# A graph layer on one Trainium2 core: the products of A2 behind the next unit's z, and the second score unit of a group between its third and fourth pair of row products

## The reference, cut to what matters

```python
h = relu(layernorm(x))
q, k, v = h @ Wq + bq, h @ Wk + bk, h @ Wv + bv
eh = edge_attr_64 @ We + be
attn_in = concatenate([q[src], k[dst], eh], axis=-1)
hmid = leaky_relu(attn_in @ A1 + b1, 0.2)
scores = leaky_relu(hmid @ A2 + b2, 0.2)        # 8 heads
w = softmax(scores.mean(axis=-1), axis=0)       # over all edges
out = segment_sum(w[:, None] * v[dst], src, num_segments=12500)
x + layernorm(h @ Wn + bn + out) * gamma + beta
```

## Time and profile before

| | |
|---|---|
| median of 3 runs | 6567.2 us (6549.49 to 6578.67) |
| the profiled execution | 6557.52 us, span 6555.7 us |
| PE, DVE, POOL, ACT busy | 76%, 63%, 49%, 46% of the span |
| mean granted clock of PE | 0.862 of full |

### The profile page before, as it was taken

How to read it: one execution, slowest core, us unless ns; L and a number is a source line. 1 busy time by engine, 2 the same in 40 slices (tenths; PEclk the granted TensorE clock), 3 DMA queues, 4 the chain that set the end, 5 groups by cost and what they waited for, 6 DMA issues and landing times. The chain is left out here.

```text
span 6555.7 us, 137361 instructions
## 1 busy us (share of the span) xinstructions
PE 4960.7 (76%) x35449; PEld 3918.0 (60%) x35449; DVE 4109.7 (63%) x9779; ACT 3008.6 (46%) x7687; POOL 3185.0 (49%) x3381
## 2 busy tenths in 40 slices
PE   7545456777878788788888887888878878879955
PEld 4433345656666666666666666666666666666754
DVE  7444444556656666566666665666666666656689
ACT  4223233444544445454445554555444445553455
POOL 3665565545555555555555555555555555520011
PEclk9777777888888888888898888888888888889999
DMA  8566666777777776666666766666666666647877
GB/s 234 151 194 201 194 190 202 210 206 212 220 218 213 224 218 187 176 194 193 188 189 193 197 192 180 190 195 195 181 182 181 190 183 192 198 134 204 229 175 184
DMA packets 1938653, 1276.41 MB, mean 195 GB/s; under 512 B 637802, under 2 KB 1830929, under 8 KB 1938444
## 3 DMA queue, kind: packets, MB, share of 16 engines
q1 hardware_dynamic: 1768101, 831.59, 50.3%
q0 software_dynamic: 154752, 435.99, 18.3%
q10 hardware_dynamic: 15592, 6.41, 0.4%
HBM read 703.28 MB, written 570.23 MB: 194 GB/s over the span
## 5 line engine op out<-in xcount | busy, mean ns | idle before, releaser
L1284 POOL DMA_INDIRECT slots<-rows,slot_i x3224 | 3098.9, 961 | 2566.4 <-ACT rows L1442 1169.9
L1339 PE MATMUL ps_row<-win,mixed 128*128 128x256 f32 x5904 | 1543.2, 406 | 150.0 <-ACT rows L1442 63.6
L1442 ACT ACTIVATE rows<-ps_row 128x512 f32<-128x512 f32 x1476 | 886.3, 600 | 1008.2 <-remote 668.6
L857 ACT ACTIVATE low<-ps_z 128x512 f32<-128x512 f32 (+1 forms) x882 | 517.9, 587 | 1801.9 <-remote 1065.7
L1339 PEld LDWEIGHTS ps_row<-win,mixed 128*128 128x128 f32 x5904 | 1127.8, 202 | 333.3 <-issue 133.7
L869 DVE TENSOR_SCALAR onehot<-ps_ls,part 128x512 bf16<-128x512 bf16 x686 | 330.3, 482 | 1429.2 <-remote 583.1
L789 PE MATMUL ps_ls<-mid,a_at 128*32 128x128 f32 x5488 | 365.3, 361 | 650.1 <-issue 524.4
L1498 ACT ACTIVATE early_v<-early_v,early_weight 128x128 f32<-128x128 f32 x2744 | 835.7, 393 | 6.1 <-DMA early_v<-slots 6.0
L1310 PE MATMUL ps_e<-ident,edges 128*128 128x128 f32 x3224 | 559.1, 298 | 361.5 <-DMA edges<-edge_attr_dram 139.6
L776 PE MATMUL ps_z<-onehot,q_bits 128*128 128x512 bf16 (+1 forms) x2646 | 795.3, 410 | 41.8 <-issue 40.2
L1310 PEld LDWEIGHTS ps_e<-ident,edges 128*128 128x128 f32 x3224 | 449.8, 157 | 587.9 <-issue 306.1
(11 more groups left out here) (220 smaller groups left out, 5177.0 us busy)
## 6 DMA issues: line engine op xcount, KB each, us to landing
u_rows<-slots SPq DMA_DIRECT2D x820, 258.0 KB, 3.2
early_v<-slots SPq DMA_DIRECT2D x686, 258.0 KB
edges<-edge_attr_dram SPq DMA_DIRECT2D x403, 256.0 KB
q_bits<-qb_tab SPq DMA_DIRECT2D x882, 96.0 KB, 3.0
slots<-no_row SPq DMA_DIRECT2D x98, 528.0 KB
slots<-rows,slot_i POOLq DMA_INDIRECT x3224
slots<-no_row SPq DMA_DIRECT2D x98, 396.0 KB
u_rows<-slots SPq DMA_DIRECT2D x134, 193.5 KB, 2.8
```

The source lines that it names most:

```text
L857: nc.scalar.activation(o.low[:, k % n, 0:w, :], o.ps_z[:, k % o.ps_z.shape[1], 0:w, :], ACT.Copy, scale=SLOPE).then_inc(o.low_ready, 1)
L1284: pool.indirect_dma_start(slots_tab[h], bass.IndirectOffsetOnAxis(slot_i[:, u, j:j + 1], 0), rows[:, u, j, :], None).then_inc(scattered[u] ...
L1339: last = pe.matmul(bank[:, j % 2, :], mixed[:, u % 2, j, :], win[:, u, :], start=True, stop=True)
L1442: nc.scalar.activation(rows[:, u, 2 * k:2 * k + 2, 0:2 * U0].rearrange("p j (a c) -> p j a c", a=2)[:, :, :, 0:D], row_bank(s, k).rearrang ...
```

## The change

In the loop over groups the batch's A2 products move from ahead of spread_lo to behind make_z of the same unit, and count on a semaphore of their own (`heads_made0`), for which raise_heads and leaky_z wait. DVE takes leaky_z ahead of one_of in the unit after a batch. On PE and on ACT the late unit moves between pair 2 and pair 3. The last batch's counts follow.

```diff
         def heads_count(o, i, k):
             if o.inside:
-                i, k = unit_of(o, i, k)
-                return i * o.units + k // BATCH * BATCH + (batch_size(o, i, k) + 2)
+                return batch_at(o, i, k) + 1
...
-                       low_ready=sem("low_ready0"), mid_ready=sem("mid_ready0"), s_ready=unit_made,
+                       low_ready=sem("low_ready0"), mid_ready=sem("mid_ready0"), s_ready=sem("heads_made0"),
...
                     def unit(i, k):                                  # PE
-                        if ended(o, i, k - 1):
-                            batch_heads(pe, o, *ended(o, i, k - 1))
                         if has_unit(o, i, k + 1):
                             spread_lo(pe, o, *unit_of(o, i, k + 1))
                         if ended(o, i, k - 2):
                             sum_heads(pe, o, *ended(o, i, k - 2))
                         make_z(pe, o, i, k).then_inc(unit_made, 1)
+                        if ended(o, i, k - 1):
+                            batch_heads(pe, o, *ended(o, i, k - 1)).then_inc(o.s_ready, 1)
...
                         if in_group(s, 0):                           # PE, both
                             make_rows(s, u, 2)
-                            make_rows(s, u, 3)
                         for n in units[late:]:
                             unit(*n)
+                        if in_group(s, 0):
+                            make_rows(s, u, 3)
                         if known(s) and s == LAST_UNIT_AT:
                             pe.wait_ge(o.scored, LAST_BODY)
-                            batch_heads(pe, o, LAST_BODY, LAST_UNIT).then_inc(unit_made, 1)
-                            sum_heads(pe, o, LAST_BODY, LAST_UNIT).then_inc(unit_made, 1)
+                            batch_heads(pe, o, LAST_BODY, LAST_UNIT).then_inc(o.s_ready, 1)
+                            sum_heads(pe, o, LAST_BODY, LAST_UNIT).then_inc(unit_made, 2)
...
                         if in_group(s, 1):                           # ACT, both
                             copy_feats(s + 1, (u + 1) % UNROLL, 1)
+                        for n in units[late:]:
+                            unit(*n)
                         if in_group(s, 0):
                             copy_rows(s, u, 3)
-                        for n in units[late:]:
-                            unit(*n)
...
                     def unit(i, k):                                  # DVE
+                        if ended(o, i, k - 1):
+                            leaky_z(dve, o, i, k)
                         if has_unit(o, i, k + 1):
                             one_of(dve, o, *unit_of(o, i, k + 1))
-                        leaky_z(dve, o, i, k)
                         if ended(o, i, k - 1):
                             keep_heads(dve, o, *ended(o, i, k - 1))
+                        else:
+                            leaky_z(dve, o, i, k)
```

## The result

The changed kernel takes 6820.87 us (median of 3 runs, 6811.35 to 6832.69) against 6567.2: 1.0367 times before, 95% interval 1.0314 to 1.0419. That is 254 us slower, outside the range of the prediction, on the side that it called the likelier, at four times the size (+60). The profiled execution takes 6832.69 us (span 6830.9), 275 more than that of before.

The account below looks back on a forecast made before the run. PE's work plus a loop of late z, held signal, ACT, DVE and PE was taken as the bound. +0.68 - 0.98 + 0.98 - 0.55 = +0.13 to +0.68 us, taken as 0.35, times 172: +60, 6618 us; range 6430 to 6730.

Parts of the forecast that it names:

- the dependence of the second pair on the fourth copy: PE's second pair of the next group waits for ACT's fourth copy, its bank free about 1.15 us after late z's signal.
- The 0.3 us of lo: Lo transposes on PE fall into the idle time before the batch, winning 0.3 us per batch.
- signal to end of batch and z: From late z's held signal until batch and next z are done: 4.08 us before, 4.76 after, +0.68.
- early z (or batch) to late z of the even step: The fourth pair of row products leaves this stretch on PE: -0.98 us.
- late z to the next early z: The fourth pair of row products now stands in this stretch on PE: +0.98 us.
- odd step: Early z to late z: -0.98 us for the pair, less 0.43 of waiting for early z's maximum; net -0.55.
- Rival 2: POOL runs out of rows, late z's signal comes up to 2.5 us sooner, kernel faster: 6455, at most 6190; chance 0.25.
- Covered, as POOL is busy for only 55%: POOL's last two scatters of odd groups start about 1.7 us later, covered by its 630.3 us of waits in 3,000.
- Rival 5: POOL starves: the 1.7 us of later scatters is passed on in each pair, +290, 6850 us; chance 0.07.
- Rival 1: PE's stall moves to the row products and costs a little: 6580 to 6675 us, likeliest 6618; chance 0.42.
- Rival 3: Row products and lo fill PE's 4.1 us of idle: -220, 6337 us, or 6447 with half the batches; chance 0.09.
- Rival 4: Nothing moves: gain and loss meet, or only PE's unchanged sum of work counts: 6557 us (6540 to 6590); chance 0.17.

Follow-up runs that it names:

- run 8: Kernel before with ACT's half of the second part alone: late scaling ahead of the fourth copy, PE's order unchanged; 6616.99 us, 1.0051 of before.
- run 9: Run 2 with POOL's last two scatters of a group reading the third pair's rows, so not waiting for the fourth copy; 7061.78 us, 1.0457 of before.
- run 2: Kernel before with the second part alone: late unit between third and fourth pair on PE and ACT, batch ahead of z; 6983.67 us, 1.0329 of before.
- run 17: Run 3's kernel again, late unit moved on PE alone, measured in one set with run 18; 6435.35 us, 0.9763 of before.
- run 7: Changed kernel with ACT's order of before, so batch behind z and late unit moved on PE only; 6475.4 us, 0.9875 of before.
- run 3: Kernel before with the late unit moved on PE alone, ACT copying the fourth pair ahead of the late scaling; 6582.63 us, 0.9743 of before.
- run 1: Changed kernel with the late unit back in its place on PE and ACT, so the first part alone; 6756.48 us, 0.998 of before.
- run 4: Kernel before with only the four lo transposes moved ahead of the batch, which stays ahead of z; 6768.5 us, 1.0012 of before.
- run 6: Kernel before with a ninth indirect scatter for each group, into a table that nobody reads; 7171.31 us, 1.0935 of before.
- run 12: Run 3 once more, late unit moved on PE alone, in the set of runs 9 to 12; 6571.02 us, 0.973 of before.
- run 13: Run 2 with POOL's first scatter of each group held until ACT is past the early unit's scaling; 6918.32 us, 1.0507 of before.
- run 14: Kernel before with POOL's first scatter of each group held until ACT is past the early unit; 7289.86 us, 1.1067 of before.
- run 16: Kernel before with the late unit ahead of both third and fourth pair on PE alone, ACT's order unchanged; 6857.75 us, 1.0432 of before.
- run 18: Run 7's kernel again, changed kernel with ACT's order of before, in one set with run 17; 6496.84 us, 0.9821 of before.

## Why the prediction was wrong

**Right:** the direction; the dependence of the second pair on the fourth copy, at 1.14 us; that PE's idle time leaves the batch (430.3 us, now 131.1) and grows at the row products (38.2, now 178.8), that DVE's one-hot no longer waits for the raise, that POOL's waits for rows grow; that the first part brings little. The 0.3 us of lo brought nothing.

**The failed step** is the sum for one pair of steps, in its terms of the even and of the odd step, "-0.98" and "-0.55". They took a pair of row products out of a stretch, took the stretch as shorter by its length, and gave ACT's new order no effect on it. The four terms, as predicted and as measured (after less before in the table):

- signal to end of batch and z: +0.68, measured +0.43. The order is right and the size near.
- early z (or batch) to late z of the even step: -0.98, measured +1.39.
- late z to the next early z: +0.98, measured +0.58.
- odd step: -0.55, measured +0.72.
- what the sum had no term for: the late z's signal comes 1.31 us sooner after its end (4.03 to 2.72). Rival 2 has the mechanism, and at least a part of it is shown: run 8, with the copy behind the signal and nothing else, has it at 2.94, and run 9, which feeds POOL its last two scatters again, has it at 2.91 instead of run 2's 2.37. The sign that rival 2 was to show, waits of ACT of 3 us or less, is absent (4.8). The gain of 1.31 is less than the error of the even step (2.4) and about that of the odd one (1.3).

With the PE half alone the two terms do come out: run 17 less before is -1.42, +0.74 and -0.61 us for the three stretches for which the sum had -0.98, +0.98 and -0.55. So what failed is not the arithmetic on PE's order, but that it was taken to hold with ACT's new order beside it. ACT's half by itself lengthens both stretches, with the first part and without: the changed kernel has 8.43 and 6.79 us where run 7, with ACT's order of before, has 6.84 and 5.69, and run 2 has 7.18 and 7.24 where run 3 has 6.03 and 6.24. The prediction priced that order by one wait, the second pair's for the fourth copy, and put at nothing what else it moves.

The even step lost most. There the prediction gave the batch's own signal "nothing" and 0.5 us if the cover went; DVE's maximum now starts 6.1 us after the early z's end (2.5 before), ACT's raise 3.0 us after the batch's (4.3 before, where lo and z stood between), and the transposes and sum behind them take 1.55 and 3.19 us instead of 0.91 and 2.52 (means of the 130 pairs). But runs 1 and 7 have that signal too (run 7 has DVE's maximum 5.3 us after z's end) and lose nothing against before, and run 2 lacks it and loses 3.3%, so the signal is one way in which the loss shows and not its cause. In the odd step z waits for a maximum whose signal is held longer than before: early z is scaled 3.1 us after its end and 2.0 before (3.6 in run 2, where run 4 has 2.25). The prediction knew of this wait, and took 0.43 us from one pair shown.

**POOL.** "Covered, as POOL is busy for only 55%" was the wrong question. POOL's share says nothing of what a scatter costs: a ninth one costs 1.15 times its own length (run 6). Rival 5 had the total nearly right (6850) and its sign, POOL's waits for rows, came close to the bound (892 of 900 us), but its way, late last scatters, is refuted: they aren't late (they start 3.3 us behind the next group's first products after, 4.0 before), and run 9, which frees them from the fourth copy, is slower. Its other mark, PE waits for rows of over 3 us in each pair, is absent: 178.8 us in some 99 pairs, 1.8 each.

**Rivals 1, 3 and 4.** Rival 1 was the mechanism seen in the trace, and not the size: a copy behind the held signal costs 0.5% (run 8), 35 us, near the +22 and +60 of the sum. Rival 3, row products that fill the stand, is what PE's half alone does (runs 3, 12 and 17: 2.4 to 2.7%, where it said 1.7 to 3.4%). Rival 4 is refuted by the same runs: PE does the same 35,449 instructions in less time (run 17).

**What is shown and what is open.** Shown: the loss comes with the second part, needs both engines' halves (0.974 and 1.005 apart, 1.033 together), and doesn't come of late last scatters, which are not late after the change, nor in run 2. The bank's wait costs little by itself (run 8); with both halves no run takes it away, so its share there is open.

In the stretches that grew PE's issue and signals are slow while POOL scatters (table and timelines): in 2,700 to 5,700 us PE has 289 gaps of 0.5 to 2 us that the profile puts down to "issue", 278 us in all, against 135 and 147 us before. They don't settle it, since run 17 has 224 with 273 us and is the fastest.

The changed kernel and runs 2, 9 and 16, which lose 3% and more, have in common that in even steps ACT copies the group's first rows soon (2.8 us after its first products started after, 2.5 in run 2, 3.1 in run 9, 3.4 in run 16; 6.7 before, 7.3 in run 17), so POOL's next burst starts at 6.1, 5.7, 6.3 and 7.2 instead of 9.3 and 9.3 us, over lo, z, transposes and sum. The kernels that lose little or nothing lie between or with before: run 8 at 4.5 and 8.1, run 1 at 5.3 and 8.7, runs 3, 7 and 18 at 5.7 to 6.0 and 8.7 to 8.8. That this is the cause was argued. The one test of it (runs 13 and 14, which put the burst later) went against it in the form tried, with a hold far longer than meant; a hold of 2 us wasn't tried. So the cause of the loss stays open. Why PE is slow while POOL scatters, the traces don't say.

## What to carry to other kernels

Where a signal is held, put work that nobody awaits in front of the stand, and leave the copies in the order in which their buffers are needed: the same move won 2.4 to 2.7% on PE alone and lost 3.3% with the consumer's order changed to match. Try the halves of a reordering by engine before the whole, since they needn't add up. And a stretch needn't become shorter by the length of what is taken out of it: with PE's half alone it did (-1.42 and -0.61 us), in the changed kernel, with ACT's order changed too, the same stretches grew (+1.39 and +0.72). Ask of each stretch what ends it, before and after, and what every changed engine puts there.

## What the runs showed of the hardware

- Signals of PE are often late beside POOL's indirect scatters (1.26 us apart) and seldom in their gaps. In run 14 a z that ends where no scatter had started for 1.3 us is scaled 0.04 us after its shown end (146 of 146 with ACT idle), and one that ends beside scatters 4.6 us after it in the mean (82). Not each is late: before, 106 of 249 that end beside scatters are over 1 us late, and the median is 0.11 us. Single signals are late by 5.4 us and 7.1 us (the batch that ends at 3005.84 after).
- In some bursts of scatters PE starts one instruction in about 1.4 us, with no wait that the profile shows (3007.03 to 3009.89 after, 3088.40 to 3089.81 in run 2). In others it works at full pace: from 3,025 to 3,031 us of the changed kernel POOL scatters five times, and PE is busy for 5.18 of the 6 us.
- A ninth scatter of 1.27 us in each of 403 groups costs 9.35%, with POOL busy for 50% of the span; it is 1.5 us a group without units and 1.6 with them.
- A fill on POOL of 0.33 us, three in a group, costs 0.9%: 47 us, of the 394 us that the fills take.
- The same kernel takes 2.7% longer in one set of runs than in another (6,762.5 and 6,581.5 us), and the ratio of run 3 to it is the same in both kinds of sets (0.974 and 0.976). The record's number of the chip doesn't decide it: chip 9 has 6,753.6 us in one set and 6,614.2 in a later one.
